# Two matrix products interleaved matmul by matmul, in a two-layer convolution kernel with batch norm

## What is computed

```python
k = jnp.einsum('ijk,imk->ijmk', hx, hy)[0]        # filters of layer 0, rank one per channel
y = jnp.fft.irfft2(u_f * k_f, s=(fft_size, fft_size))[..., :L, :L]
out = y + x * bias[:, None, None]
...
scores = jnp.einsum('bpsd,bptd->bpst', x, x) * inv_dim
red = jnp.sum(scores * weights[None], axis=-1, keepdims=True)
y = x + red
mean = jnp.mean(y, axis=(0, 2, 3), keepdims=True)
var = jnp.var(y, axis=(0, 2, 3), keepdims=True)
y_hat = (y - mean) * jax.lax.rsqrt(var + BN_EPS)
return y_hat * gamma[None, :, None, None] + beta[None, :, None, None]
```

## Time and profile before

| | us |
|---|---|
| median of 3 runs | 945.83 (945.75 to 945.91) |
| the profiled execution | 944.98 |
| its span | 943.1 |
| PE / DVE / ACT / POOL busy | 926.8 / 740.7 / 679.5 / 672.0 |
| TensorE clock granted | full level (2.4 GHz) outside the ends |
| DMA busy, 60 to 900 us | 89% |

### The profile page before, as it was taken

How to read it: one execution, slowest core, us unless ns; L and a number is a source line. 1 busy time by engine, 2 the same in 40 slices (tenths; PEclk the granted TensorE clock), 3 DMA queues, 4 the chain that set the end, 5 groups by cost and what they waited for, 6 DMA issues and landing times.

```text
span 943.1 us, 18642 instructions
## 1 busy us (share of the span) xinstructions
PE 926.8 (98%) x5308; PEld 812.2 (86%) x5308; DVE 740.7 (79%) x2197; ACT 679.5 (72%) x1092; POOL 672.0 (71%) x526
## 2 busy tenths in 40 slices
PE   8999999999999999999999999999999999999994
PEld 6888888888888888888888888888888888888884
DVE  2778788778878878878878878887887887887886
ACT  4447777777777777777777777777777777677676
POOL 2777677777777777767767767777777776776763
PEclk9999999999999999999999999999999999999998
DMA  7778998798989999888898999969899999988944
GB/s 241 256 222 188 292 258 270 285 254 255 285 252 268 261 282 268 292 242 266 254 267 287 214 289 299 290 231 288 220 280 301 270 226 306 268 243 291 262 131 201
DMA packets 91454, 244.15 MB, mean 259 GB/s; under 512 B 17200, under 2 KB 41904, under 8 KB 83248
## 3 DMA queue, kind: packets, MB, share of 16 engines
q1 hardware_dynamic: 73440, 235.53, 82.9%
q10 hardware_dynamic: 18000, 8.46, 3.7%
HBM read 176.59 MB, written 67.37 MB: 259 GB/s over the span
## 4 chain that ended last, share of the span: by engine, by line
PE 96%; ACT 1%; DMA 1%; DVE 1%; POOL 0%; issue 0%; SPq 0%; DVEq 0%; POOLq 0%
PE ps_c L638 36%; PE ps_u L638 32%; PE ps_z L638 28%; DMA toep_whole<-filters_padded 1%; ACT z_sb L589 0%; DVE z_sb L850 0%; POOL zl L490 0%; ACT uh L520 0%; DMA filters_padded<-z_sb 0%; DVE ul L889 0%; DVE z_sb L783 0%; ACT z_sb L624 0%; ACT zh L614 0%; DVE products L863 0%; ACT z_sb L512 0%
## 5 line engine op out<-in xcount | busy, mean ns | idle before, releaser
L490 POOL TENSOR_TENSOR zl<-z_sb,zh 128x1024 fp32r<-128x1024 f32 x127 | 303.5, 2390 | 239.1 <-ACT zh L614 239.0
L863 DVE CUSTOM_DVE_ANT_0 products<-z_sb,ps_c 128x256 bf16<-128x256 f32 x504 | 182.2, 418 | 159.9 <-PE ps_c L638 159.9
L638 PE MATMUL ps_z<-uh,toep 128*128 128x512 f32 x768 | 271.4, 408 | 0.4 <-DVE z_sb L850 0.2
L520 ACT ACTIVATE uh<-ps_u 128x1024 fp32r<-128x1024 f32 x127 | 130.5, 1028 | 183.4 <-PE ps_u L638 183.4
L589 ACT ACTIVATE out_sb<-z_sb,shift,gain 128x256 f32<-128x256 f32 x496 | 257.2, 591 | 5.5
L638 PE MATMUL ps_u<-toep,xh 128*128 128x256 f32 x1016 | 234.8, 312 | 1.0 <-DVE ul L889 0.8
L638 PE MATMUL ps_c<-zh,wh 128*128 128x512 f32 x504 | 196.2, 389 | 0.1
L638 PE MATMUL ps_c<-zl,wh 128*128 128x512 f32 x504 | 196.1, 389 | 0.0
L638 PE MATMUL ps_c<-zh,wl 128*128 128x512 f32 x504 | 196.1, 389 | 0.0
L638 PE MATMUL ps_u<-toep_whole,xt_sb 128*128 128x128 f32 x1016 | 195.2, 273 | 0.0
L614 ACT ACTIVATE zh<-z_sb 128x1024 fp32r<-128x1024 f32 x127 | 134.7, 1061 | 54.5 <-DVE z_sb L850 50.3
(11 more groups left out here) (95 smaller groups left out, 903.5 us busy)
## 6 DMA issues: line engine op xcount, KB each, us to landing
xt_sb<-xt_in SPq DMA_DIRECT2D x64, 1024.0 KB, 10.3
x_sb<-x_in SPq DMA_DIRECT2D x128, 512.0 KB, 8.2
out<-out_sb SPq DMA_DIRECT2D x124, 512.0 KB, 6.7
w_sb<-wt_in SPq DMA_DIRECT2D x64, 256.0 KB, 7.3
toep_whole<-filters_padded SPq DMA_DIRECT2D x63, 256.0 KB, 7.4
everyone<-partition_moments ACTq DMA_DIRECT2D x62, 128.0 KB, 8.9
out<-z_sb SPq DMA_DIRECT2D x2, 512.0 KB, 2.8
partition_moments<-own ACTq DMA_DIRECT2D x62, 1.0 KB, 5.8
```

The costliest lines, as they stand in the source:

```text
L490: nc.gpsimd.tensor_tensor(low, z_sb[:, r, h], high.bitcast(F32), ALU.subtract)\
L520: nc.scalar.activation(uh[:, us.slot(2)], u_bank(us)[:, :, :, :], ACT.Copy)\
L638: return nc.tensor.matmul(o, a, b, start=start, stop=stop)
L863: last = nc.vector.tensor_tensor_reduce(products[:, cs.slot(2), k, b], z_sb[:, r, h, k, b], bank[:, k, b], 1.0 / math.sqrt(SIDE), 0.0, ALU ...
```

## The change

- TensorE: in a step the first product (pair s-2) and the third now alternate, matmul by matmul, in a new function `products_u_and_c`; all waits of both stand ahead of its first matmul. The second product follows.
- The third product works one pair later (`LAG_RED` 5), and w's rounding and its load move with it (`LAG_W` 3, `LAG_LOAD_W` 5). `LAG_W` being odd, ACT and POOL now round w in the same step as the Toeplitz block.
- `ps_u` gets four banks, two pairs of two by turns; `ps_avg` lies in the second pair. The first product now waits for the `ul` of two pairs before.
- DVE: the sums of the third product (`reduce_rows`) come first in a step, ahead of `ul`; `mean_of_partition` moves from ahead of `ul` to behind the statistics.
- ACT: the gather moves from behind the norm of the even step to behind the Toeplitz block of the odd step (`LAG_GATHER` 7). The spread keeps its place in the odd step. POOL: the sum of the means moves behind w's low part.
- At the end of the run the third product of pair 124 is no longer cut into two halves around the second product.

```diff
-LAG_W, LAG_U, LAG_Z, LAG_RED = 2, 2, 3, 4
-LAG_MEAN = 6
+LAG_W, LAG_U, LAG_Z, LAG_RED = 3, 2, 3, 5
+LAG_MEAN, LAG_GATHER = 6, 7
...
-LAG_LOAD_XT, LAG_LOAD_T, LAG_LOAD_W, LAG_LOAD_X = 1, 3, 3, 5
+LAG_LOAD_XT, LAG_LOAD_T, LAG_LOAD_W, LAG_LOAD_X = 1, 3, 5, 5
...
-        ps_u = ps("ps_u", [P, BLOCKS, PAIR, SIDE])
+        ps_u = ps("ps_u", [P, 2, BLOCKS, PAIR, SIDE])
...
-        ps_avg = ps("ps_avg", [P, 2, SIDE * PAIR])
+        ps_avg = ps_u[:, 1].rearrange("p k b w -> p k (b w)")
...
-            return ps_c if second_pair(us) else ps_u
+            return ps_u[:, us.slot(2)]
...
+                ms = st.trail(LAG_GATHER)
+                if starts(ms) and not ending(ms, 4):
+                    r = ms.ring(XR)
+                    wait_chan(act, mean_in, ms, 1)
+                    nc.scalar.dma_start(own_dram[r:r + 1, :].rearrange("o (p n) -> (o p) n", n=2), own[:, r])\
+                        .then_inc(gathered, 16)
...
+            def products_u_and_c(us, cs):
+
+                r, t, s, w = us.ring(XR), us.ring(2), us.slot(4), cs.ring(2)
+                wait_chan(pe, wl_ready, cs, 1)
+                wait(pe, zl_ready, cs, 1)
+                wait(pe, red_ready, cs, 0)
+                if us.first_of_channel():
+                    wait_chan(pe, tl_ready, us, 1)
+                wait(pe, xl_ready, us, 1)
+                wait(pe, ul_ready, us, -1)
...
+                for i in range(BLOCKS):
+                    for j in range(PAIR):
...
+                        mm(c, w_h, high[:, j], j == 0, False)
+                        mm(u, x_h, t_h, True, False)
+                        mm(c, w_h, low[:, j], False, False)
+                        mm(u, x_h, t_l, False, False)
+                        last = mm(c, w_l, high[:, j], False, j == BLOCKS - 1)
+                        if i == j == BLOCKS - 1:
+                            last.then_inc(c_done, 1)
+                        mm(u, x_l, t_h, False, False)
+                        last = mm(u[:, P:SIDE], xt_sb[:, r, PAIR * us.half() + j, 1, rows],
+                                  toep_whole[:, r, 1, 0:P], False, True)
+                last.then_inc(u_done, 1)
```

More of the change, by code:

```diff
@@ L437, in stage @@
             def stage(st):
-                ms = st.trail(LAG_MEAN)
-                if starts(ms) and not ending(ms, 4):
-                    shift_means(ms)
                 def low_toeplitz(ts, parts):
@@ L591, in stage @@
                     last.then_inc(norm_done, 1)
-                ms = st.trail(LAG_MEAN)
-                if starts(ms) and not ending(ms, 4):
-                    r = ms.ring(XR)
-                    wait_chan(act, mean_in, ms, 1)
-                    nc.scalar.dma_start(own_dram[r:r + 1, :].rearrange("o (p n) -> (o p) n", n=2), own[:, r])\
-                        .then_inc(gathered, 16)
                 ss = st.trail(LAG_SPREAD)
@@ L705, in stage @@
                     wait(pe, xl_ready, us, 1)
-                    if not second_pair(us):
-                        wait(pe, ul_ready, us, 0)
+                    wait(pe, ul_ready, us, -1)
                     s = us.slot(4)
@@ L726, in stage @@
                     product_y(zs)
-                cs = st.trail(LAG_RED)
-                if st.static() and st.number() >= PAIRS:
-                    late = Step(0, PAIRS - 4)
-                    wait(pe, red_ready, late, 0)
-                    product_c(late, ps_c, [st.number() - PAIRS])
-                elif active(cs):
-                    wait(pe, red_ready, cs, 0)
-                    product_c(cs, ps_c)
             run_steps(pe, PAIRS, UNROLL, END_STEPS, stage)
@@ L760, in _ @@
             product_y(end[2])
-            product_c(end[0], ps_u)
+            product_c(end[0], ps_u[:, 0])
             pe.wait_ge(red_ready, PAIRS - 3)
@@ L880, in stage @@
                     gain_and_offset(gs)
-                ms = st.trail(LAG_MEAN)
-                if starts(ms):
-                    mean_of_partition(ms)
+                cs = st.trail(LAG_RED)
+                if active(cs):
+                    reduce_rows(cs, ps_c)
                 us = st.trail(LAG_U)
@@ L894, in stage @@
                     whole_z(zs)
-                cs = st.trail(LAG_RED)
-                if st.static() and st.number() >= PAIRS:
-                    if st.number() == PAIRS + 1:
-                        gain_and_offset(Step(0, PAIRS - 8))
-                        reduce_rows(Step(0, PAIRS - 4), ps_c)
-                elif active(cs):
-                    reduce_rows(cs, ps_c)
                 if active(zs) and not ending(zs, 2):
                     statistics(zs)
+                ms = st.trail(LAG_MEAN)
+                if starts(ms):
+                    mean_of_partition(ms)
                 vs = st.trail(LAG_TOTAL)
@@ L948, in _ @@
             statistics(end[1])
-            reduce_rows(end[0], ps_u)
+            reduce_rows(end[0], ps_u[:, 0])
             statistics(end[2])
@@ L954, in _ @@
             mean_and_variance(before)
-            reduce_rows(end[2], ps_u, last_red)
+            reduce_rows(end[2], ps_u[:, 0], last_red)
             whole_variance(before, 2)
```

29 lines of the change are left out of this document (20 added, 9 removed).

## The result

| | before | after |
|---|---|---|
| median (us) | 945.87 (945.75 to 946.71) | 1032.3 (1026.5 to 1044.0) |
| ratio | | 1.089 (95%: 1.0865 to 1.0919) |
| the profiled execution, its span | 944.98, 943.1 | 1026.52, 1024.7 |

What follows compares the result with a forecast made beforehand. TensorE's gapless matmul stream was taken as the bound. From 944.98 us, -8 for interleaving, +27 for gather stalls and +1.5 at the tail gave 965.5, with 0.85 for the median 966; range 934 to 990.

Steps and rivals of the forecast that it cites:

- Part 3: Channel's mean: gather issued 3.5 us later, ACT stops at the spread, zh late, TensorE stalls above 6.75 us landing: +27 us.
- I take w's 7.3, the nearest in time: Gather's landing time when issued amid SP's loads: taken as w's 7.3 us, bounds 2.9 and 9.8.
- a steady excess costs half of itself: TensorE's stall for one chain is slack for the next, so the 0.55 us excess costs 0.27 per channel.
- The longer step thins the burst and takes some back: DMA traffic around the gather: stalls lengthen the step, offsetting some of the scatter's cost; no separate size given.
- Its clock staying at the full level: TensorE's clock: expected to remain at full level despite about 27 us of stalls; no cost included.
- Part 1: Alternating first and third products on TensorE: 256-column matmuls get faster, 0.065 us a step, -8 us; bounds 0 and 13.6.
- has no row for it: Loss from alternating PSUM banks on TensorE: the profile's starts show no step at bank changes, so none was priced.
- Part 2: New places of sums, uh, ul, zh, zl and the Toeplitz block: no stall, cost 0; thinnest slack 0.5 us.
- Part 4: Run's ends: head unchanged; at the tail 1.8 us idle before the last second product instead of 0.3, +1.5 us.
- A: Gather's packets served beside SP's, landing in 3 to 6 us without delaying TensorE: 939 us; chance 0.29.
- C: On TensorE the interleaving gives nothing and nothing stalls: 947 us; chance 0.06.
- D: DVE's totals, waiting for the late spread, hold up the sums: 20 us, 958 if the other wait is absent; chance 0.06.

Runs made afterwards that it cites:

- e9_late_gather_statistics_first: Kernel before, with DVE's statistics and own moved ahead of the third product's sums and ACT's gather issued behind the odd step's Toeplitz block: 1050.7 us.
- e3: Kernel before, with the gather behind the odd step's Toeplitz block and mean_of_partition behind sums and statistics: 1312.8 us, ratio 1.388.
- e4: Changed kernel with the alternation undone: all twelve matmuls of the third product, then the first product's four places; waits kept: 1013.0 us, ratio 1.0671.
- e5: Kernel before with only ACT's gather moved, to between xh and the Toeplitz block of the odd step: 955.5 us, ratio 1.0092.
- e8: Changed kernel with SP's loads of the Toeplitz block and of w issued one step earlier: 1053.9 us, ratio 1.1179.
- e12: Changed kernel with ACT rounding z to zh before it waits for the gather and issues the spread: 987.8 us, ratio 1.0424.
- e1: Changed kernel with the channel's mean early again: own behind ul, gather behind the even step's norm: 954.6 us, ratio 1.0105.
- e6: Changed kernel with the mean and gather early again and the alternation undone, third product's matmuls before the first's: 947.7 us, ratio 1.0022.
- e11: Kernel before with the first product reordered: twelve 256-column matmuls first, then the four in plain float32: 947.9 us, ratio 1.0022.
- e2_moments_before: Changed kernel whose spread reads and waits for the gather of the channel before, everything else in place: 954.5 us, ratio 1.009.
- e10: Changed kernel with SP's loads of w and the Toeplitz blocks cut to 8 columns a row from the seventh channel on: 953.4 us, ratio 1.0091.
- e13: Changed kernel with the gather's DMA left out from the ninth channel's step on, norm using old moments: 952.0 us, one execution.

## Why the prediction was wrong, point by point

**Part 3, mechanism: right.** Gather issued at 5.33 where nothing had delayed it (forecast 5.43), ACT still at the spread, and zh, zl and the joined product late by over 0.3 behind 37 of the 62 gathers. Of chains whose gather went out at 5.3, read one by one, the stall follows from the landing:

| landing | stall before it | own stall | landing - 6.88 - stall before |
|---|---|---|---|
| 7.81 | 0 | 0.96 | 0.93 |
| 8.52 | 0 | 1.70 | 1.64 |
| 9.28 | 0 | 2.39 | 2.40 |
| 9.09 | 0.46 | 1.68 | 1.75 |
| 9.29 | 0.23 | 2.12 | 2.18 |

The limit was forecast as 6.75 and is 6.88, and a stall is slack for the next chain, as written.

**Part 3, size: wrong, in two terms.** The forecast had 27 us of stall; measured are 58 and 12 of clock. With the recurrence of the table (limit 6.87), over 60 channels:

- Landing 7.3 each, on time: 13 us, and 16 by the forecast's own limit. The rest of its 27, some 11, stood for scatter.
- Landing at the real mean of these 60, 8.1: 37. The yardstick was w's 7.3, taken with the gather out of the way. With the gather in the middle w itself takes 9.1. The step that failed is "I take w's 7.3, the nearest in time": the row was right and the moved DMA changed it.
- Each landing as measured: 50. Scatter counts 13, about what was allowed for it.
- Each issue as measured: 67, against the 58 seen. This is the second step that failed, "a steady excess costs half of itself". A late zh delays all that ACT does after it, uh and through it ul, z and own too, so the next gather goes out later than 5.3, by 0.7 in the mean, and eats up the slack that the stall had given. In e9_late_gather_statistics_first the issue slips by 1.5, and the same sum gives 92 with it and 54 without, for 79 seen: that is why it is worse than the changed kernel. Why its issue slips more wasn't tried.
- "The longer step thins the burst and takes some back" found no support: landing didn't fall.

**The clock: not in the sum at all.** "Its clock staying at the full level" was wrong. Counted in the loop of the seven kernels with stalls (the changed one, e3, e4, e5, e8, e9, e12), of 149 gaps of 0.3 to 2 us one was followed by a stretch at half clock, of 48 of 2 to 3 us 27, and of 69 longer ones 63. In the changed kernel it was 7 of the 11 above 2 us, while its gap of 3.8 us at 745.8 was followed by none; 52 of all come from e3_late_gather, so the share differs much by kernel (7 of 15 in e9). A stretch cost 1.6 to 1.8 us: 12 us here, 91 in e3_late_gather. The forecast's mean stall of 0.45 hid that those which make up the sum are of 1 to 4 us.

**Part 1: wrong sign.** +7.0 us (e1 against e6) instead of -8. The 256 columns did get faster, from 0.1190 in the mean to 0.1175, which gives back 18 ns a step, about a quarter of the 65 that the forecast took. The step that failed is that the 512 columns would keep their 0.227. One place of the changed kernel, TensorE in time:

```profile
212.11 0.48 PE L639 MATMUL ps_c<-zh,wh 128*128 128x512 f32 x1
212.42 0.28 PE L639 MATMUL ps_u<-toep,xh 128*128 128x256 f32 x1
212.54 0.39 PE L639 MATMUL ps_c<-zl,wh 128*128 128x512 f32 x1
212.77 0.28 PE L639 MATMUL ps_u<-toep,xh 128*128 128x256 f32 x1
212.89 0.40 PE L639 MATMUL ps_c<-zh,wl 128*128 128x512 f32 x1
213.13 0.28 PE L639 MATMUL ps_u<-toep,xl 128*128 128x256 f32 x1
```

From 212.54 to 212.77 and from 212.89 to 213.13, a matmul of 512 columns holds 0.23 to 0.24. By the ends of the matmuls over all undisturbed steps it is 0.2327 in the mean against 0.2267: 12 x 6.0 = +72 ns, the 256 columns give back 18 and the plain ones 5, together +0.05 a step. The second product didn't recover its 0.03 either: its nine take 2.077 in both. The forecast put a loss by alternating at nothing because it "has no row for it"; with no row, the lower end should have been a loss and not 0. What makes the 512 columns slower stays open. A change of bank alone doesn't: the first matmul of the third product follows the second's at 0.227 in the kernel before. Nor is it only the other shape, since the second product's nine take 0.227 to 0.235 each by their place, with 512 columns on both sides of all but the first. The Trainium skill (TensorE: Matmul & The Clock Gate, "LDWEIGHTS") was nearer with its gain of none, though 256 columns every 0.120 (e11) are slower than both of its figures, and no figure there gives the loss.

**Part 2: right.** In e2_moments_before, with all moved instructions in place and no stop, gaps of TensorE are 4 us in all. The slack of 0.5 of the Toeplitz block was thin indeed: the block became a bound in e12.

**Part 4: right.** The wait ahead of the last second product in the changed kernel (forecast 1.8 idle, +1.5; the end of the run is 1.5 longer in e1 than in the kernel before):

```profile
PE ps_z L639 <- DVE z_sb L874: 1.6, 1, 1.6
```

**The sum.** From the forecast's 965.5 to the profiled 1026.5 are 61 us: 31 more of stall, 12 of clock, 14 of alternation (+5.8 instead of -8) and 4 to 5 in smaller pieces. The median lies 6 higher still; the four executions scatter by 17 us.

**The rivals.** A (the gather slips past) fell: it lands in turn with what SP issued ahead of it (e8, e10). The Trainium skill's turns between queues (DMA: Bandwidth & Descriptors, "Queues, rings and completion order") don't help a transfer here; its sentence that a semaphore lands behind the engine's earlier writes fits better, though no run separates the two. C fell too: the alternation costs, and there are stalls. D, in the changed kernel, shows as 21.3 us of DVE waiting for the spread, covered by the other stall; its price becomes visible in e12.

The forecast's far end, 92 us of stall, was set aside as needing "every landing at the most ever seen". With the feedback by ACT and the clock most of it came about with a landing of 8.

No version beats the kernel before. The best of the new order, e6, is 0.1 to 0.3% slower, with the same step.

## What to carry to other kernels

A wait that stands in an engine's order is priced by what is queued behind it: work out the limit of the landing, and if the typical landing is near it, count the feedback (the late engine issues the next transfer late) and the clock that long stalls can cost on top, not half of the mean excess. Here the landing of a tiny DMA went with the traffic issued ahead of it, and moving it into a burst also slows the burst, so no row of before is a safe yardstick: keep such a DMA ahead of the burst, or let nobody wait for it in order. And the matmuls' cost changed with what stood beside them: bound an interleaving on both sides, and try it with everything else in its old place.

## What of the hardware was not expected

- A DMA of 1 KB in 128 packets of 8 bytes delayed the loads around it, 1.75 MB, by 2.2 to 2.7 us and the stores by 3.7, and raised the DMA engines' busy share from 83 to 92% (e13, e2).
- ACT's queue issued a DMA ahead of the end of the activations before it in the code: 0.08 behind the start of zh, with xh still to come (e5).
- 256-column matmuls follow each other every 0.120 (e11), behind 512 columns they take 0.113 to 0.122, and the third product's 512 columns next to 256 take 0.229 to 0.239 instead of 0.227 (e1); plain float32 of 128 columns costs 0.109 to 0.112 for each of its two records in every order.
- Stretches at half clock came behind most gaps of over 3 us (63 of 69), about half of those of 2 to 3 us (27 of 48) and hardly ever behind shorter ones (1 of 149).
